# A fused layernorm, attention and feed-forward kernel: the score stream moved by one step and the exponential stream by four

## The reference

```python
x = L0_attn_x
x = x + 0.5 * _L0_ffn_ref(_layernorm(x), ...)
x = x + _L0_attn_ref(_layernorm(x), ...)
x = x + 0.5 * _L0_ffn_ref(_layernorm(x), ...)
...
# attention
q = _rope(q)
k = _rope(k)
scores = jnp.einsum('bhqd,bhkd->bhqk', q, k) * SCALE
scores = jnp.where(tok_mask[None, None], scores, -jnp.inf)
attn = jax.nn.softmax(scores, axis=-1)
ctx = jnp.einsum('bhqk,bhkd->bhqd', attn, v)
...
# feed-forward: layernorm, then weights rounded to -1, 0, 1, plus a bias
return jnp.einsum('bsi,oi->bso', xn, w_q) + bias
```

## Time and profile before

| What | Value |
|---|---|
| Time, median of 3 runs (lowest to highest) | 634.64 us (634.29 to 636.09) |
| The profiled execution | 634.23 us, span 632.4 us |
| PE busy | 554.8 us, 88% of the span |
| DVE busy | 396.8 us, 63% |
| ACT busy | 310.2 us, 49% |
| POOL busy | 238.5 us, 38% |
| Chain that ended last | PE 56%, DVE 19%, issue 8%, POOL 7%, DMA 7%, ACT 3% |

### The profile page before, as it was taken

The page is one execution under the profiler, slowest core; times in us unless marked ns, Lnnn a source line. Parts: engine busy times, 40 slices in busy tenths (PEclk is TensorE's granted clock), DMA queues, the critical chain, the costliest instruction groups (busy, mean ns, idle before and its releaser), DMA issues.

```text
span 632.4 us, 10042 instructions
## 1 busy us (share of the span) xinstructions
PE 554.8 (88%) x3586; PEld 235.9 (37%) x3586; DVE 396.8 (63%) x782; ACT 310.2 (49%) x629; POOL 238.5 (38%) x200
## 2 busy tenths in 40 slices
PE   0695799679969999999999999999999898999876
PEld 0442445334423333333333333333333334344432
DVE  5899656626767757757757657657657843431672
ACT  0931632121215746746746746746736548572320
POOL 4001363443474646646646646646600100000100
PEclk9796899888989999999999999999999999999997
DMA  8921023354221215423213214514410003100011
GB/s 322 348 76 68 2 70 97 117 119 133 93 83 51 77 52 175 127 67 110 76 51 109 77 52 150 169 51 143 138 57 2 1 2 134 51 18 34 33 68 66
DMA packets 43601, 57.95 MB, mean 92 GB/s; under 512 B 3526, under 2 KB 34374, under 8 KB 42528
## 3 DMA queue, kind: packets, MB, share of 16 engines
q1 hardware_dynamic: 42972, 57.21, 27.6%
q10 hardware_dynamic: 580, 0.11, 0.1%
HBM read 32.01 MB, written 25.17 MB: 90 GB/s over the span
## 4 chain that ended last, share of the span: by engine, by line
PE 56%; DVE 19%; issue 8%; POOL 7%; DMA 7%; ACT 3%; SPq 1%; ACTq 0%; POOLq 0%; DVEq 0%
PE bank L956 9%; PE bank L874 7%; PE bank L939 7%; PE bank L920 7%; PE bank L1045 6%; PE bank L1055 5%; PE bank L884 5%; PE bank L993 5%; DMA kst<-spread 4%; DVE rmax L815 4%; DVE mparts L828 3%; DVE stats L661 3%; POOL rot L502 2%; DMA spread<-rhl 2%; PE bank L864 2%
## 5 line engine op out<-in xcount | busy, mean ns | idle before, releaser
L815 DVE TENSOR_REDUCE rmax<-bank 128x1 f32<-128x512 f32 (+3 forms) x384 | 200.9, 553 | 124.5 <-PE bank L939 121.5
L609 ACT ACTIVATE big<-bank 128x512 f32<-128x512 f32 (+3 forms) x384 | 182.0, 490 | 150.6 <-PE bank L920 145.7
L939 PE MATMUL bank<-kst,qst 104*128 104x512 f16 (+3 forms) x384 | 126.3, 330 | 15.3 <-issue 8.5
L920 PE MATMUL bank<-qst,kst 106*128 106x512 f16 (+3 forms) x384 | 123.9, 330 | 2.5 <-ACT big L609 2.2
L502 POOL TENSOR_TENSOR rot<-t,sin_s 64x512 f32<-64x512 f32 x64 | 81.8, 1277 | 96.3 <-ACT t L602 93.5
L1045 PE MATMUL bank<-big,ones 128*32 128x512 f32 (+3 forms) x768 | 81.8, 498 | 0.0
L1055 PE MATMUL bank<-big,rows 128*32 128x512 f32 (+3 forms) x768 | 79.5, 486 | 0.0
L920 PEld LDWEIGHTS bank<-qst,kst 106*128 106x128 f16 x384 | 37.1, 97 | 84.4 <-issue 41.4
L511 POOL TENSOR_TENSOR rhl<-t,rhl 128x512 f16<-128x512 f32 x32 | 37.5, 1171 | 70.9 <-ACT rhl L623 70.9
L521 POOL TENSOR_TENSOR cl<-cf,ch 128x512 f16<-128x512 f32 x16 | 18.6, 1160 | 112.3 <-ACT ch L641 112.3
L939 PEld LDWEIGHTS bank<-kst,qst 104*128 104x128 f16 x384 | 37.8, 98 | 51.2 <-issue 18.9
(11 more groups left out here) (106 smaller groups left out, 667.9 us busy)
## 6 DMA issues: line engine op xcount, KB each, us to landing
spread<-rhl SPq DMA_DIRECT2D x32, 256.0 KB, 2.2
qst<-spread SPq DMA_DIRECT2D x16, 384.0 KB, 3.8
kst<-spread SPq DMA_DIRECT2D x16, 384.0 KB, 3.8
x<-rows SPq DMA_DIRECT2D x4, 1024.0 KB, 4.6
spread<-rhl SPq DMA_DIRECT2D x32, 128.0 KB, 2.1
rows<-in_L_attn_x_dram SPq DMA_DIRECT2D x3, 1024.0 KB, 15.5
xh<-ch SPq DMA_DIRECT2D x4, 512.0 KB, 4.6
xl<-cl SPq DMA_DIRECT2D x4, 512.0 KB, 6.2
```

The costliest lines, as they stand in the source:

```text
L609: nc.scalar.activation(probs[:, st % P_PLACES, h, 0:n], pb[u % 2][:, 0:n], ACT.Exp, scale=EXP_SCALE).then_inc(s_eb, 1)
L815: nc.vector.tensor_reduce(rmax[:, at:at + 1], a_bank(u)[:, 0:n], AX.X, ALU.max, negate=True).then_inc(s_max, 1)
L920: nc.tensor.matmul(pb[u % 2][:, 0:n], kst[0:ROWS_B, g % SETS, h, j * P:(j + 1) * P], qst[0:ROWS_B, g % SETS, h, q0:q0 + n], start=True, st ...
L939: nc.tensor.matmul(a_bank(u)[:, 0:n], qst[0:ROWS_A, g % SETS, h, i * P:(i + 1) * P], kst[0:ROWS_A, g % SETS, h, half * HALF:half * HALF + ...
```

## The change

Four places are edited. The score stream starts one step later and the exponential stream four steps later, while the projections, and the feed-forward and output work that stands at fixed steps, stay. The transpose of a head's maxima, with ACT's copy and SP's DMA behind it, stands five steps after the head's last score instead of two. It now comes after u4 of the next head, so its bank may hold a tile that DVE has yet to read, and a wait for that is added.

```diff
-A_START, B_START = 10, 18
+A_START, B_START = 11, 22
-MAX_PLACE = 2
+MAX_PLACE = 5
...
-                if e := max_head(k, 4):
+                if e := max_head(k, MAX_PLACE + 2):
...
-                if e := max_head(k, 3):
+                if e := max_head(k, MAX_PLACE + 1):
...
                     pe.wait_ge(s_mp, n + 1)
+                    if n + 1 < GH * ALL:
+                        pe.wait_ge(s_max, A_UNITS * (n + 1) + MAX_PLACE - 2)
                     nc.tensor.transpose(max_bank(n)[0:2 * TILES, 0:P // 2].bitcast(F16),
```

## The result

The changed kernel takes 636.33 us (median of 20 runs, 634.37 to 640.41), the kernel before beside it 634.12 us (20 runs, 632.81 to 636.09). The ratio is 1.0039, interval 1.0027 to 1.0052: slower by 0.39%, some 2.2 us by the medians and 2.5 by the ratio. The forecast was 5.35 us slower. After's profiled execution took 636.18 us (span 634.4), 1.95 us above before's 634.23 (span 632.4).

A forecast was written before the change was run, and what follows sets the result against it. PE was taken as the bound in full stream. On 634.23 us, +2.3 (stream) - 0.4 (first groups) + 1.95 (end) + 1.5 (ACT beside feed-forward) = +5.35 gave 639.6 us; range 631 to 647.

The forecast's parts named there:

- Line 825 and line 828: At a head's end, POOL's `rot` holds both; DVE is held 0.5 us longer, u3 stalls 1.15 us in second heads.
- The waits that go: PE's stall at the transpose (line 1063) goes, and its waits for the transfer into `kst`, 4.7 us, are won.
- The end: At the last context, one feed-forward tile no longer covers the 3.87 us chain: +1.95 us, bounds 0 and 2.2.
- First groups and ACT beside the feed-forward tiles: First two groups: net -0.4 us; wider exponentials and a logarithm beside batch 0's feed-forward tiles: +1.5, bounds 0 and 2.5.
- Sum in the stream: Under 23 heads with projections and exponentials, stalls 13.4 us against 6.4 plus 4.7 before: net +2.3, bounds 0 and +7.
- the 11.1 us that before loses under the 23 heads: In the stream, the kernel before's waits: 6.4 us for the transpose and 4.7 for the transfer into `kst`.
- the 13.4 of after: In the stream, new stalls on u3: 6 x 0.95 + 6 x 1.15 + 5 x 0.15 = 13.4 us.
- can win or lose only PE's idle time, 1.75 us in such a group: Groups in full stream: PE is the bound, busy 45.54 of 47.29 us, so order affects only its idle 1.75.
- slip through: First rival, at a head's end: line 825 is not held by `rot`, PE never stalls at u3; 626.2 us, chance 0.14.
- is not held: Line 827, one SBUF input, runs free of POOL; the second rival had it held too: 668.6 us, chance 0.05.
- The third rival: In the stream, DVE's stalls equal what PE lost before, 11.1 us, other costs covered: 634 to 635 us, chance 0.18.

The follow-up runs named there:

- The reduction: The changed kernel with line 825 as a minimum over pairs that reads SBUF once, the maxima stored in pairs: 621.81 us, ratio 0.9809.
- Putting the tile back: The changed kernel with batch 0's last four feed-forward tiles four steps later, one again behind the last value product: 634.02 us, ratio 0.9992.
- the kernel at 651.87: The kernel before with score stream (11) and exponential stream (22) moved, the transpose still two steps behind the head's end: 651.87 us, ratio 1.0283.

## Why the prediction was right in direction and wrong in size

**Line 825 and line 828.** Right. Both are held, each to the end of a half of `rot`, and u3 starts within 0.02 us of the forecast. The reduction shows the cause: with one SBUF input line 825 takes 0.16 under the same `rot`, and the stall on u3 is gone with it. The Trainium skill's page "SBUF — State Buffer", section "Who interferes with whom", says that `tensor_reduce` never contends with POOL on this chip; the trace agrees: 28 of the 32 begin under a POOL instruction, and none takes more than 0.16 us.

**The waits that go.** Right. The transpose and `kst` have left PE's waits (9.9 and 4.7 us before).

**The end.** Right as far as it went: 1.95 forecast, 2.05 measured. It left out the clock. The eight matmuls at 0.42 us instead of 0.22 cost 3.37 - 1.73 = 1.64 (eight matmuls before took from 588.72 to 590.45), the main part of the 2.0 behind the wait. Putting the tile back brought 3 us. The lower clock's price is not fixed: behind the same wait of 3.52 us the granted clock over the next 3 us was 0.72 in the kernel at 651.87 and 0.70 in the one at 621.81.

**First groups and ACT beside the feed-forward tiles.** -0.4 + 1.5 = +1.1 forecast; what is left of the streams outside the five groups is +1.31. That the two agree is luck, as PE's recorded waits show. Between the first copy and the twelfth they fall from 20.0 to 19.6 us: -0.4, as forecast, though from other parts (u4's waits give back 2.1 instead of 0.9, and waits for line 815 come to 6.2 where the transpose's were 4.8). Behind the last copy PE waits for exponentials 2.2 us in both kernels, so nothing of the +1.5 shows there; in its place a wait of 1.0 us for DVE's line 676 ahead of line 864 is new.

**The step that failed: "Sum in the stream".** It gave +2.3 us; the five groups in full stream brought -2.19. The places were right and the sizes were not set on one scale: the term for what before loses to its waits was too small. After's stalls were worked out along PE's path (2.25 a group), before's were taken from the recorded idle time (1.07 + 0.69). The stall-free group of 44.88 us gives both on one scale: before lost 47.29 - 44.88 = 2.41 us a group, after 46.86 - 44.88 = 1.98. Recorded idle is 1.75 and 1.49. In the sum's own terms, the 11.1 us that before loses under the 23 heads were 23/4 x 2.41 = 13.9, the 13.4 of after were 23/4 x 1.98 = 11.4, and the step came to -2.5.

So the sentence that an order "can win or lose only PE's idle time, 1.75 us in such a group" was wrong. A change of order can also make PE's own path longer, as the transpose's new place does by itself. Why recorded idle time is too little the rows of before show: a matmul of 512 columns is recorded as busy for 0.38 us but stands only 0.22 on the path, so the first 0.16 of a stall behind it read as busy. Before has four waits in a group (0.35, 0.67, 0.04 and 0.69 us), and (2.41 - 1.75) / 4 = 0.165. After has two recorded ones (0.64 and 0.85) and a third, in the fourth head, that is not recorded at all:

```profile
322.79 0.27 PE L920 MATMUL bank<-qst,kst 106*128 106x256 f16 x1
323.05 0.38 PE L939 MATMUL bank<-kst,qst 104*128 104x512 f16 x1
```

A tile of 256 columns stands 0.11 on the path, so this u3 came 0.15 late, the figure that the prediction has for it.

By 2.41 against 2.25 the same step would have given 23/4 x -0.16 = -0.9, and a total near +2.1. That this is near what was measured would have been luck too: the clock is not in it, nor the 1.19 us ahead of the change, and the +1.5 is. The other part is that the stalls after were a little smaller than worked out, 1.98 for 2.25: the first head's u3 waits to 334.10, PE's path there ended at 333.29, 0.81 for 0.95.

**The rivals.** Line 825 did not slip through. Line 827 did not meet POOL in the changed kernel, since it begins in the short gap between the halves of `rot` (343.95, against 342.63 + 1.31 = 343.94). That it "is not held" was wrong all the same: in the kernel with the reduction it begins under POOL 28 times and takes 0.40 to 0.94 us. The same section of the Trainium skill counts `tensor_scalar` among the operations that can contend, and the experiment agrees. The third rival, the stall only moves, came nearest in time, and it described the stream better than the forecast did; but it wanted the end covered, and the end was lost as forecast.

**The new place of the transpose alone.** Its group lies 2.41 us above the stall-free one with 1.14 of recorded idle time in it. The transpose's place on PE accounts for about 0.8, and its two recorded waits hide some 0.16 each. What is left, about 0.1, was not traced to its instructions.

## What to carry to other kernels

Compare stalls on one scale: the period of a loop that has none, or the path of the matmuls, and not recorded idle time on one side, which leaves out about 0.16 us of each stall here. Before moving a matmul of another shape, compare also the distances from start to start around its old and its new place: here the place of a transpose made 0.2 us a head without any wait. When a short vector instruction with two SBUF inputs meets POOL's long ones, rewrite it to read SBUF once and let it start under them; the order then decides whether that pays. When cover is taken from a wait on PE, price the wait and also what PE's clock does behind it.

## What the runs showed of the hardware that was not expected

A DVE `tensor_scalar` from 32 to 16 bits on 128 by 8 elements, with one SBUF input, took 0.62 us under a POOL instruction instead of 0.17, and ended with it; so it went in all 28 heads in which it began under one (0.40 to 0.94 us). Between two POOL instructions in a row DVE can start an instruction that would otherwise be held: in the kernel with the reduction line 828, with two SBUF inputs, took 0.17 us in all 32 heads; in the head shown it started 0.03 us behind the end of the first half of `rot`, ahead of the second.

A transpose behind a projection matmul instead of behind value products took 0.2 us more of PE's path, its neighbours counted, with no wait recorded.

After 3.52 us without a matmul PE's granted clock over the next 3.3 us was 0.51 in the changed kernel; after 1.47 us, in the kernel before, it was 1.00. The length of the wait alone did not decide it: a wait of 1.78 us for line 815 was followed by 0.51 in the kernel with the reduction and by 1.00 in the changed kernel. The first row is the one with the reduction, the second the changed kernel:

```profile
483.26:486.26 3.00, 3.00 (x15) 0.81 (x19) 2.90 (x7) 1.11 (x2) 1.60 (x2) 0.51 0.00 0
494.73:497.73 3.00, 3.00 (x22) 0.93 (x23) 2.93 (x6) 1.21 (x3) 1.60 (x2) 1.00 0.00 0
```
